# Attention, mixture of experts, linear attention and a routed LoRA layer on one core: the first four heads' stacks from the parts on chip

## The reference

```python
# layer 1: attention with rotary embedding, 16 heads of 8 features, T = 512
q = q * cos + rotate_half(q) * sin
k = k * cos + rotate_half(k) * sin
attn = softmax(einsum('bhqd,bhkd->bhqk', q, k) / sqrt(8))
out = einsum('bhqk,bhkd->bhqd', attn, v) @ W_out + b_out
# layer 2: 16 experts of 64, grouped routing (2 of 4 groups, 4 experts), and a shared expert
# layer 3: linear attention, features elu(x @ random_matrix) + 1
# layer 4: x @ W.T + b plus 2 of 8 rank-16 LoRA experts
```

## Time and profile before

| what | value |
|---|---|
| median of three runs | 461.15 us (460.24 to 461.73) |
| profiled execution | 462.07 us, of which the profile's span is 460.2 us |
| PE busy | 427.8 us (93%) |
| VectorE busy | 368.2 us (80%) |
| ScalarE busy | 241.1 us (52%) |
| POOL busy | 104.1 us (23%) |
| granted clock of PE | 0.983 of full speed over the span |

### The profile page before, as it was taken

How to read it: one execution, slowest core, us unless ns; L and a number is a source line. 1 busy time by engine, 2 the same in 40 slices (tenths; PEclk the granted TensorE clock), 3 DMA queues, 4 the chain that set the end, 5 groups by cost and what they waited for, 6 DMA issues and landing times. The chain is left out here.

```text
span 460.2 us, 7561 instructions
## 1 busy us (share of the span) xinstructions
PE 427.8 (93%) x2555; PEld 210.7 (46%) x2584; DVE 368.2 (80%) x1000; ACT 241.1 (52%) x452; POOL 104.1 (23%) x103
## 2 busy tenths in 40 slices
PE   8988989999899999999898999999999999998892
PEld 3333223223342334233232456665766675685671
DVE  6369988888798998999975298898886897887566
ACT  1502666876768776777578612236336623643320
POOL 9793052530528100200010000200120022003022
PEclk9979989999999999999999999999999999999997
DMA  4774524233351226331004122232031102000001
GB/s 143 257 192 145 156 59 113 61 104 89 84 164 35 84 76 153 116 121 32 18 7 94 25 69 90 82 80 70 24 91 48 47 32 82 25 1 24 1 1 47
DMA packets 24866, 36.16 MB, mean 79 GB/s; under 512 B 2678, under 2 KB 16246, under 8 KB 24822
## 3 DMA queue, kind: packets, MB, share of 16 engines
q1 hardware_dynamic: 24828, 35.67, 26.7%
HBM read 23.94 MB, written 11.53 MB: 77 GB/s over the span
## 5 line engine op out<-in xcount | busy, mean ns | idle before, releaser
L1136 DVE TENSOR_REDUCE negmax<-psum 128x1 f32<-128x512 f32 x256 | 163.5, 684 | 31.4 <-PE psum L536 31.0
L837 ACT ACTIVATE probs<-psum 128x512 f32<-128x512 f32 x256 | 137.4, 600 | 47.7 <-PE psum L551 40.5
L536 PE MATMUL psum<-KS,QS 125*128 125x512 bf16 x256 | 99.1, 390 | 8.1 <-DMA QS<-stack_dram 3.2
L551 PE MATMUL psum<-QS,KS 128*128 128x512 bf16 x234 | 88.0, 384 | 3.8 <-ACT probs L837 2.7
L566 PE MATMUL psum<-probs,VA 128*32 128x512 f32 x512 | 68.8, 609 | 0.3 <-ACT probs L837 0.3
L816 PE MATMUL psum<-xT,late 128*128 128x512 f32 x144 | 68.8, 600 | 0.0
L551 PEld LDWEIGHTS psum<-QS,KS 128*128 128x128 bf16 x256 | 24.6, 98 | 78.1 <-ACT probs L837 55.4
L458 POOL TENSOR_SCALAR var<-mv 128x4 f32<-128x4 f32 x16 | 3.6, 227 | 242.5 <-DVE mv L1043 242.4
L966 ACT ACTIVATE QS<-psum 128x512 f32<-128x512 f32 x36 | 21.6, 600 | 51.6 <-PE psum L816 51.6
L803 PEld LDWEIGHTS psum<-late,QS 128*128 128x128 f32 x288 | 35.7, 191 | 15.2 <-issue 10.2
L536 PEld LDWEIGHTS psum<-KS,QS 125*128 125x128 bf16 x256 | 25.4, 99 | 36.8 <-DVE negmax L1136 15.2
(11 more groups left out here) (146 smaller groups left out, 539.2 us busy)
## 6 DMA issues: line engine op xcount, KB each, us to landing
stack_dram<-parts SPq DMA_DIRECT2D x24, 384.0 KB, 3.4
cw<-w_dram SPq DMA_DIRECT2D x32, 256.0 KB, 3.2
KS<-stack_dram SPq DMA_DIRECT2D x16, 288.0 KB
QS<-stack_dram SPq DMA_DIRECT2D x16, 288.0 KB
late<-in_late SPq DMA_DIRECT2D x6, 330.5 KB, 4.6
res<-in_x SPq DMA_DIRECT2D x4, 256.0 KB, 5.8
w_dram<-wT SPq DMA_DIRECT2D x4, 256.0 KB, 4.3
out_y<-KS SPq DMA_DIRECT2D x4, 256.0 KB, 2.3
```

The source lines that it names most:

```text
L536: mm(sm_bank(u)[:, :], QS[b % 2][0:KROW, h, qt * P:(qt + 1) * P], KS[b % 2][0:KROW, h, :], start=True, stop=True).then_inc(sm_full, 1)
L551: mm(ps[v % 3][:, :], KS[b % 2][0:KROW + 3, h, kt * P:(kt + 1) * P], QS[b % 2][0:KROW + 3, h, :], start=True, stop=True).then_inc(s_full, 1)
L837: fn(probs[:, n % 2, j, :], ps[v % 3][:, :], ACT.Exp, scale=float(DH) ** -0.5).then_inc(exp_done, 1)
L1136: V.tensor_reduce(out=negmax[:, G % 4, i:i + 1], in_=sm_bank(u)[:, :], axis=X, op=ALU.max, negate=True).then_inc(sm_free, 1)
```

## The change

In batch 0 the partitions of the parts are ordered by groups of four heads, and within a group by feature and head: partitions 0 to 31 hold the first four heads. Its weights, biases and tables have that order too and come from an input of their own (`begin`, which lies in the end of `late`'s memory until `late` is loaded); `early` keeps the tables and weights of the later batches, loaded behind them (`rest_ld`), with the exchanged weights left out.

The stacks of the first four heads are no longer read from `stack_dram`. 18 DMAs copy 32 partitions of a part (32 KB) into 8 rows of the stack: nine for k, issued by SyncE, three ahead of each part's stores, and nine for q, issued by ScalarE, three behind each pair of roundings. PE waits for all 18 (`first_ld`) instead of two landings, and POOL's first batch-1 operation too. Six loads of batch 0 are left instead of eight. 28 dummy matmuls stand where there were 42. In `split_max` the two conversions are multiplications by a column of ones.

```diff
-            for a, z_, done in (("w_kq", "w_kq", rope_ld), ("b_rope", "sin", table_ld), ("w_v", "bv_row", early_ld)):
-                cols = slice(EARLY_AT[a][0], EARLY_AT[z_][1])
-                sp.dma_start(early[:, cols], early_in[:, cols]).then_inc(done, 16)
+            n = 4 * D
+            sp.dma_start(begin[:, 0:n], begin_in[:, 0:n]).then_inc(rope_ld, 16)
+            sp.dma_start(begin[:, n:], begin_in[:, n:]).then_inc(table_ld, 16)
+            n = EARLY_AT["bv_row"][1]
+            sp.dma_start(early[:, 0:n], early_in[:, 0:n]).then_inc(early_ld, 16)
             sp.dma_start(xT[:, T:2 * T], xT_in[:, T:2 * T]).then_inc(x_ld, 16)
+            sp.dma_start(early[:, n:], early_in[:, n:]).then_inc(rest_ld, 16)
...
+                if b:
+                    src = stack_dram[b, i, :, h0:h1, :]
+                else:
+                    src = stack_dram[b, i].rearrange("(r d) h t -> r (d h) t", d=DH)[:, HW * g:HW * (g + 1), :]
+                    src = src.rearrange("r (d k) t -> r d (k t)", k=HG)
+                sp.dma_start((KS, QS)[i][b % 2][0:SROW, h0:h1, :], src).then_inc(qk_ld[b % 2][g], 16)
+
+            def first_heads(p):
+
+                sp.wait_ge(split_done[0], p + 1)
+                sp.wait_ge(pad_pool, 1)
+                for y in range(3):
+                    at = 3 * DH * p + DH * y
+                    sp.dma_start(KS[0][at:at + DH, 0:HG, :], parts[0:HW, 0, p, :]).then_inc(first_ld, 16)
...
             for p in range(3):
+                first_heads(p)
                 for i in range(2):
                     store_part(0, i, p)
-            for g in range(NG):
+            for g in range(1, NG):
...
                 pool.wait_ge(parts_st[i], 48 * b)
+                if b == 1:
+                    pool.wait_ge(first_ld, 16 * 18)
...
                 if i == 0:
-                    pe.wait_ge(qk_ld[b % 2][G % NG], 32 * (b // 2 + 1))
+                    if G:
+                        pe.wait_ge(qk_ld[b % 2][G % NG], 32 * (b // 2 + (G % (2 * NG) > 0)))
+                    else:
+                        pe.wait_ge(first_ld, 16 * 18)
...
-            keep_warm(42)
+            keep_warm(28)
...
+            def first_heads(p):
+
+                act.wait_ge(split_done[1], p + 1)
+                for x in range(3):
+                    at = 3 * DH * x + DH * p
+                    act.dma_start(QS[0][at:at + DH, 0:HG, :], parts[0:HW, 1, p, :]).then_inc(first_ld, 16)
+
+            act.wait_ge(pad_dve, 1)
             for p in range(2):
                 for i in range(2):
                     act.wait_ge(vsum_done, 2 * p + i + 1)
                     fn(parts[:, i, p, :], rot[:, 2 * i, :], ACT.Copy).then_inc(split_done[i], 1)
+                first_heads(p)
+            first_heads(2)
             for s in ropes[4:]:
                 beside_act(*s)
...
-                yield from after(V.tensor_copy(o[:, 0, :], v))
+                yield from after(tt(o[:, 0, :], v, plus1[:, 0:1].to_broadcast([P, HG * NT]), ALU.mult))
                 yield from after(tt(r, v, o[:, 0, :], ALU.subtract))
-                yield from after(V.tensor_copy(o[:, 1, :], r))
+                yield from after(tt(o[:, 1, :], r, plus1[:, 0:1].to_broadcast([P, HG * NT]), ALU.mult))
```

More of the change, by code:

```diff
@@ L65 @@
 WARM = {("x2T", 3): 2, ("x3T", 3): 13, ("ghT", 3): 2, ("O", 3): 4, ("AT", 3): 3, ("KT", 3): 1}
-EARLY = dict(w_kq=4 * D, b_rope=4, cos=T, sin=T, w_v=D, ident=P, bv_row=D)
+BEGIN = dict(w_kq0=4 * D, b_rope0=4, cos0=T, sin0=T)
+EARLY = dict(w_v=D, ident=P, bv_row=D, w_kq=2 * D, b_rope=2, cos=T, sin=T)
 LATE = dict(w_out=D, bout_row=D, wg=E0, reset16=NT * E0, reset8=NT * E1, w1=E0 * F0, w3=E0 * F0, w2=EP * D, w1s=D, w3s=D, w2s=D,
@@ L79, in columns @@
     return out, at
+BEGIN_AT, BEGIN_N = columns(BEGIN)
 EARLY_AT, EARLY_N = columns(EARLY)
@@ L85, with program @@
 LATE_PIECES = 8
-def program(nc, x_in, xT_in, early_in, late_in, identb_in, ones_in, stack_dram, w_dram, out):
+def program(nc, x_in, xT_in, begin_in, early_in, late_in, identb_in, ones_in, stack_dram, w_dram, out):
     with ExitStack() as ctx:
@@ L99, in program @@
         c_.update({k: late[:, a:b] for k, (a, b) in LATE_AT.items()})
+        begin = late[:, LATE_N - BEGIN_N:LATE_N]
+        c_.update({k: begin[:, a:b] for k, (a, b) in BEGIN_AT.items()})
         ident = c_["ident"]
@@ L168, in program @@
         split_done = [sem(f"split_done{i}") for i in range(2)]
+        first_ld, rest_ld = sem("first_ld"), sem("rest_ld")
         parts_st = [sem(f"parts_st{i}") for i in range(2)]
@@ L337, in load_stack @@
                 sp.wait_ge(parts_st[i], 48 * (b + 1))
-                if b < 2 and g == 0:
+                if b == 0 and g == 1 or b == 1 and g == 0:
                     if i:
@@ L364, in load_late @@
                     return
+                if j == 1:
+                    sp.wait_ge(rot0_done, 4)
                 n = LATE_N - LATE_FIRST
@@ L506, in _ @@
             pool.wait_ge(pad_pool, 3)
-            pool.wait_ge(table_ld, 16)
+            pool.wait_ge(rest_ld, 16)
             for i in range(2):
@@ L652, in beside_pe @@
                         pe.wait_ge(x_ld, 16 * min(b, 2))
-                    last_ = mm(o[:, :], c_["w_kq"][:, m * D:(m + 1) * D], xT[:, b * T:(b + 1) * T], start=True, stop=True)
+                        pe.wait_ge(rest_ld, 16)
+                    w_ = c_["w_kq"][:, m // 2 * D:(m // 2 + 1) * D] if b else c_["w_kq0"][:, m * D:(m + 1) * D]
+                    last_ = mm(o[:, :], w_, xT[:, b * T:(b + 1) * T], start=True, stop=True)
                 if kind == "val":
@@ L854, in beside_act @@
                     wait_full(act, u)
+                    act.wait_ge(rest_ld, 16)
                     act.wait_ge(split_done[m // 2], 3 * a)
-                    fn(rot[:, m, :], bank_of(u)[:, :], ACT.Identity, bias=c_["b_rope"][:, m:m + 1])
+                    fn(rot[:, m, :], bank_of(u)[:, :], ACT.Identity, bias=c_["b_rope"][:, m // 2:m // 2 + 1])
                     lo, hi = slice(0, P // 2), slice(P // 2, P)
-                    fn(rot[lo, m + 1, :], bank_of(u)[hi, :], ACT.Identity, bias=c_["b_rope"][hi, m:m + 1])
-                    fn(rot[hi, m + 1, :], bank_of(u)[lo, :], ACT.Identity, bias=c_["b_rope"][lo, m:m + 1]).then_inc(rot_done, 1)
+                    fn(rot[lo, m + 1, :], bank_of(u)[hi, :], ACT.Identity, bias=c_["b_rope"][hi, m // 2:m // 2 + 1])
+                    fn(rot[hi, m + 1, :], bank_of(u)[lo, :], ACT.Identity, bias=c_["b_rope"][lo, m // 2:m // 2 + 1]).then_inc(rot_done, 1)
                 if kind == "KV":
@@ L1269, in _ @@
                     wait_full(dve, ("rope", 0, m))
-                    V.scalar_tensor_tensor(out=rot[:, m, :], in0=ps[m][:, :], scalar=c_["b_rope"][:, m:m + 1],
-                                           in1=c_["cos"] if m % 2 == 0 else c_["sin"],
+                    V.scalar_tensor_tensor(out=rot[:, m, :], in0=ps[m][:, :], scalar=c_["b_rope0"][:, m:m + 1],
+                                           in1=c_["cos0" if m % 2 == 0 else "sin0"],
                                            op0=ALU.add, op1=ALU.mult).then_inc(rot0_done, 1)
@@ L1343 @@
     order = f % H * DH + f // H
-    partner = f % H * DH + (f // H + DH // 2) % DH
     d = f // H
@@ L1352 @@
     sign = np.where(d < DH // 2, -1.0, 1.0)[:, None]
-    early = dict(w_kq=np.concatenate([wk[:, order], wk[:, partner], wq[:, order], wq[:, partner]], 1), w_v=wv,
-                 b_rope=np.stack([b_k[order], b_k[partner], b_q[order], b_q[partner]], 1),
-                 cos=np.cos(ang).astype(np.float32), sin=(np.sin(ang) * sign).astype(np.float32),
+    cos, sin = np.cos(ang).astype(np.float32), (np.sin(ang) * sign).astype(np.float32)
+    d0 = f % HW // HG
+    head0 = f // HW * HG + f % HG
+    order0, partner0 = head0 * DH + d0, head0 * DH + (d0 + DH // 2) % DH
+    begin = dict(w_kq0=np.concatenate([wk[:, order0], wk[:, partner0], wq[:, order0], wq[:, partner0]], 1),
+                 b_rope0=np.stack([b_k[order0], b_k[partner0], b_q[order0], b_q[partner0]], 1),
+                 cos0=cos[d0 * H], sin0=sin[d0 * H])
+    early = dict(w_kq=np.concatenate([wk[:, order], wq[:, order]], 1), w_v=wv, b_rope=np.stack([b_k[order], b_q[order]], 1),
+                 cos=cos, sin=sin,
                  ident=np.eye(P, dtype=np.float32), bv_row=rows(bq[2 * D:]))
@@ L1381 @@
         "in_x": np.ascontiguousarray(x), "in_xT": np.ascontiguousarray(x.T),
+        "in_begin": np.ascontiguousarray(np.concatenate([begin[k] for k in BEGIN], 1)),
         "in_early": np.ascontiguousarray(np.concatenate([early[k] for k in EARLY], 1)),
```

2 lines of the change are left out of this document (removed).

## The result

| | kernel before | changed kernel |
|---|---|---|
| median | 459.25 us (20 runs, 457.67 to 461.79) | 462.09 us (20 runs, 460.31 to 464.14) |
| ratio | | 1.0053, 95% interval 1.0035 to 1.0071: slower by 2.4 us (the two medians lie 2.8 apart) |
| span of the profiled execution | 460.2 us | 459.2 us |

The two profiled executions stand the other way round from the medians, and this matters for how all that follows is read. The 20 runs of the kernel before have a median 1.9 us under the three from which the prediction started. In its profile PE's clock fell twice before the last 10 us, in that of the changed kernel once. So I compare places of the trace (first score, split, first exp) over the profiles of several kernels with the same start, and take the time from the ratios.

What follows compares the result with a forecast made beforehand. It took PE as the bound, 93% busy, with time won at the start kept to the end. Start 2.0 us gained, split 0.0, conversions -0.1 hidden: 461.15 - 2.0 = 459.2 us; forecast 458.3 to 460.3, full range 456.3 to 462.6.

Steps and rivals of the forecast that it cites:

- The start, the main term: First score tile, without the round trip through stack_dram: at 23.1 us instead of 25.1, 2.0 us gained.
- 18.4 + 9c: Time of the first score after batch 1's six ScalarE copies, put off by nine issues of c, taken as 0.52 us.
- Rival 1: ScalarE's issues cost 0.73 to 0.8 us, first score at 25.0 to 25.6, no change: 461.0 to 461.6 us; chance 0.18.
- The landings: Last of SyncE's small k copies issued at 18.6, landed between 21.1 and 23.0 us, hidden by ScalarE's copies.
- rival 3: Cheap ScalarE issues of 0.31 us, landings bind at 21.1 to 22: 3 to 3.9 us gained; chance 0.12.
- The split of group 0: First split of the maxima: one operation held 1.0 us by POOL's tensor_tensor against today's 1.0, so 0.0 gained.
- rival 5: POOL's tensor_scalar also holds VectorE in the first split, up to 1.49 us more: 460.7 us; chance 0.03.
- the new wait for the tables: Added tables loaded behind xT delay batch 1's rope matmuls by at most 1 us, covered by copies coming 4.6 later.
- Covers: Work moved later stays covered: group 1's stacks near 28.5 us, needed by the 17th tile at about 33, 4 us cover.
- rival 2: ScalarE's nine issues held by a full queue at 1.10 us each, first score 28.3, slower: 464.3 us; chance 0.09.
- Rival 4: Group 2's split misses POOL at 61.7 and the clock's fall goes: 2.0 + 2.0 + 1.7 gained, 455.5 us; chance 0.13.

Runs made afterwards that it cites:

- g4: Kernel before with nine spare copies of the change's shape issued by ScalarE to memory nobody reads yet, POOL's batch-1 work waiting for them; ratio 1.0104.
- f2: Changed kernel with ScalarE's nine issues behind its roundings and batch 1's six copies, SyncE's nine ahead of most stores, 37 dummy matmuls for 28; ratio 1.0099.
- e3: Changed kernel with the two conversions of the maxima's split put back in place of the multiplications; ratio 1.0070 to the kernel before.
- e1: Changed kernel with 50 dummy matmuls ahead of the first score instead of 28; ratio 1.0063 to the kernel before.
- f1: Changed kernel with two unused columns that put cos and sin back at their former place within 512 bytes; ratio 1.0075 to the kernel before.
- e2: Kernel before with 28 dummy matmuls instead of 42, nothing else of the change; ratio 1.0013.
- g1: Changed kernel, batch 1's copies ahead of ScalarE's issues, batch 0's six stores behind the 18 small copies, three q issues on SyncE, 34 dummies; ratio 1.0101.
- f7: Kernel before with POOL's first batch-2 operation made to wait for the end of group 2's split of the maxima; ratio 0.9983.
- f4: Kernel before with 126 unused columns putting cos and sin at the changed kernel's place within 512 bytes; ratio 1.0011.

## Why the prediction was wrong

**The start, the main term.** The formula held: first score at 18.4 + 9c. The step that failed is the size of c, the time of one issue on ScalarE. I took 0.52 from the cw copies; ScalarE's issues took 0.68 at least, 1.28 the first, 1.2 one in a full queue, with their gaps 0.85 on average. The roundings were 0.65 us earlier than in the profile of before, so 18.4 - 0.65 + 9 x 0.85 = 25.4, as measured. Rival 1 named this and the row nearest in kind, maxp with 0.73; I had both in hand and chose the cheaper on the argument that runs were fewer and longer. g4 shows that nine such copies issued by ScalarE are enough to make the kernel slower.

**The landings.** They failed by the same size, on SyncE. Forecast: the last small copy issued at 18.6 and landed between 21.1 and 23.0, hidden by ScalarE's copies. Measured: issued at 21.33 and landed at 24.25, since SyncE's nine took 0.67 at least and up to 1.1. In the changed kernel ScalarE still ended last. But with short issues on ScalarE alone the first score would have come at 24.25, level with the 24.4 of the kernel before, so with SyncE's issues as they were rival 3's 3 to 3.9 us weren't there to be had. f2 shows it: its copies ended at 18.0, and its first score came at 25.9.

**The place compared with.** 25.12 was one execution's first score. The five other profiles with the start of before have 23.7 to 24.5. Against their 24.4 the changed kernel is 1.0 late, where I had 25.12 to 23.1 as 2.0 early. Of the term's 3.0 us, 2.3 are the issues and 0.7 this base. Counted from ScalarE's first rounding, which starts at 8.9 to 10.1 in these profiles, the first score comes after 14.4 to 15.0 us in the upper six and after 15.9 in the three of the changed kernel in which ScalarE's copies release it: 0.9 to 1.5 late.

**The split of group 0.** Forecast: one operation held 1.0, no difference. Measured: 1.87 to 2.16 over four profiles against 0.83 to 1.80 over six, about 0.7 more. POOL started at 25.17, not 22.5, since SyncE's own nine issues put off the last stores; the first operation met a tensor_tensor as forecast, and a second lost 0.3 in a tensor_scalar, which rival 5 had at up to 1.49. That the later start of POOL makes the split longer is read from the rows; no run moved POOL's start alone. That multiplications are held like conversions was right (e3, and 1.24 at 36.77).

**Not in the prediction.** The place of cos and sin in memory, and with it the split of group 4: 0.85 more there, 0.35 less in group 2. And the new wait for the tables: I gave it at most 1 us and it was 1.66, covered as said by ScalarE's lateness, but PE's idling there can bring the clock down, as in e1 and f1.

**The sum.** 2.0 at the first exp and 0.4 at groups 2 and 4 make 2.4, as the ratio has it (1.6 to 3.3). Of the 2.0, 1.0 are in the first score and 0.7 in the split; the rest is open. All are read from few profiles each, so that they meet the ratio so closely is in part luck. How much of it is the clock is open too: in the changed kernel's profile it fell from 22.8 to 29.6 us, and e1 and e2 bound the effect of the dummies at about 0.3% either way, no finer.

**Covers.** Group 1's stacks were covered, as forecast, only because the first score was late. In g1, where the first score came at 21.9, the 17th tile waited 4.1 us for them and the transposition came 6.1 us after the split. Part of that is g1's own order, with all six stores behind 12 small copies of SyncE. In the changed kernel group 1's stacks had landed by 31.5, where the prediction had 28.5, so of the 4 us of cover that it found for a first score at 23.1, about 1.5 were there; it didn't count that SyncE's issues would take 0.67 instead of 0.52 each, nor that the regrouped loads would take 0.73 to 0.84 instead of 0.31 to 0.37.

**Chances.** Slower by more than 0.3% had 0.09, in rival 2, by the issues in a full queue at 0.9 us or more. The mechanism was rather rival 1's: seven of the nine issues took 0.68 to 0.87, the first 1.28 and one, in a full queue, 1.21. Their 0.85 on average would have given 0.9 us slower by the formula; the split and groups 2 and 4, which rival 2 didn't have, did the rest. That its case came true in the size was luck. Rival 4's price was right in place and less in size: POOL's collision at 61.7 is worth 2.0 in the trace and about 0.8 us in the medians (f7), whose interval reaches from 2.1 faster to 0.5 slower and so doesn't exclude the 2.0.

## What to carry to other kernels

An issue is work of the engine that issues it. A copy that folds partitions into fewer rows cost 0.67 us per issue here and up to 1.3, so nine of them on ScalarE and nine on SyncE put the first score at 25.4, behind the 24.4 of the stores and loads through DRAM that they replaced. Count the issues on every engine that has some: moving ScalarE's behind its urgent work (f2) gained nothing, because the landings stood next. Fewer and larger copies were not tried. When a start is shortened, follow the next group through the old path before taking the gain: here the 17th tile stood in PE's order ahead of what the first exp needs. And take the base of a comparison from more than one profile when a clock can fall in one and not in the other.

## What the runs showed of the hardware

- A tensor_tensor of POOL over 128 x 512 float32 took 1.27 us or 1.09, with nothing changed but the place of one operand and of what lies behind it: 504 bytes further in f4 (1.09 for 1.27), 8 bytes further in f1 (1.27 for 1.09). No other places were tried.
- A multiplication of VectorE with a column of ones in SBUF was held until the end of POOL's tensor_tensor (1.24 at 36.77), as a conversion is (1.18 at 37.02).
- The first DMA that ScalarE issued took 1.26 to 1.32 us in all eight profiles that have one, most of the later ones 0.68 to 0.72.
- Loads of a stack took SyncE 0.73 to 0.84 us an issue in the changed kernel where they had taken 0.31 to 0.37, with the DRAM side regrouped from 72 rows to 9 x 8: the same bytes into the same rows, twice the time of an issue.
